# A graph-attention layer on one core: new order of the first loads, the query product in column tiles, and another order of the last frame's scores

## The chip, the cores and the metric

The kernel runs on one NeuronCore of a Trainium2 chip, as a single launch. TensorE (PE in the profile) multiplies matrices and writes to PSUM; VectorE (DVE), ScalarE (ACT) and GpSimd (POOL) do the elementwise work; SyncE (SP) issues nearly all DMAs. Each engine runs its own list of instructions in order, and they wait for each other by semaphores. The metric is the time on the device in microseconds, as the median of several runs.

## The reference, cut to what matters

For 16 frames (B) of 512 rows (N) and 512 features (F), with one query row of 512 numbers per frame:

```python
row_zero = v.sum(-1) == 0
q_exp = jnp.where(row_zero[..., None], 0.0, q[:, None, :])
self_feat = concatenate([v, q_exp], -1) @ W_self.T + b_self      # W1 acts on v, W2 on q
output = self_feat
for d in range(2):                                               # two directions of the edges
    A = adj_f if d == 0 else swapaxes(adj_f, 1, 2)
    cond, vb = A[:, :, :20].sum(-1), A[:, :, :20] @ w_bias + b_bias
    kv = self_feat[:, :20]                                       # 20 keys per frame
    qh, kh = self_feat @ Wq[d].T + bq[d], kv @ Wk[d].T + bk[d]   # 16 heads of 32
    aff = einsum('bnhd,bmhd->bnhm', qh, kh) / sqrt(32)
    w = softmax(where(cond > 0, aff, -9e15) + vb, axis=-1)
    out_t = einsum('bnhm,bmf->bnhf', w, kv)
    output = output + einsum('bnhf,hgf->bnhg', out_t, Wout[d]) + bout[d]
return v + relu(output)
```

## The kernel before

Every fp32 product is made from two parts of each operand: a high part (a copy by ACT, `wkh`, `w1h`, `woh`, `xh`) and a low part (the difference, `wkl`, `w1l`, `wol`, `xl`), and three products of them (`parts`, lines L513 to L515). A copy to the high part is ACT's, the subtraction for the low part is DVE's or POOL's.

**Prologue** (about the first 72 us). SP issues all loads in one list. PE first runs 11 products of ones (`warm`), then `query`: the 16 query rows times W2, as four plain fp32 products of `qT` (16 columns per chunk of 128 features) that add up in one PSUM bank. `key_self_feat` follows: the sums of the keys' rows (L443, L444), the query turned into columns by four transposes (L436, after ACT has copied it as `qrow`), and the keys' self features for all 16 frames, 320 columns (16 times 20), as 48 products into four banks of `aff`: first chunks 0 and 1 of the features for all four outputs f, then chunks 2 and 3 for one f after the other. DVE multiplies the query into the rows that are not zero (`sfkv`, L1082), adds the products (`key_feat`, L1091), ACT makes the high part with the bias (`key_feat_high`, L811), DVE the low one (`key_feat_low`, L1099). `keys` multiplies them by Wk: 32 products with `wkh` and 16 with `wkl`, then four groups of 12, each of which waits until DVE has taken a bank (`key`, L1054). `values` multiplies them by Wout and needs `wol` of chunk f at its f-th step, and all but one of the keys taken. Then come the first frame's self features and its products of keys and Wq (`g`).

**Frames.** The lists of all engines are written out by hand, so that frame n = b+1's self features are computed beside frame b's softmax. A frame has four tiles of 128 rows; a tile's `scores` are 24 products with 320 columns (3.5 us), for which the two banks of `aff` serve in turn. After a tile's scores DVE adds the bias and takes the maximum (`shift`, L1033 and L1035), POOL subtracts the maximum (`sub_max`, L1265), ACT takes the exponential (L882), DVE sums and inverts (`total`), POOL multiplies (`normalise_rest`, `normalise`). PE transposes the weights and multiplies them by the values (`attend_rest`, `attend`). DVE then adds the self features (`add_sf`, L1017), ACT applies the ReLU (`relu`), POOL issues a DMA that adds x in place (`add_x`, L1293), and SP stores the result one frame later (`store_out`, L367).

`ahead` is the number of frames that are still to come, at most 2: it is 1 in frame 14 and 0 in frame 15. The last frame has a list of its own: its tile 3 is scored in two halves (`last_scores`), DVE subtracts that tile's maximum itself (`last_sub_max`) and normalises it (`last_normalise`), and the result is stored in four parts (L405) as it comes.

## Time and profile before

| | us |
|---|---|
| median of 3 runs | 594.58 (592.99 to 594.88) |
| profiled execution, time | 593.21 |
| profiled execution, span of the core | 591.4 |
| PE busy in the span | 580.8 (98%) |
| DVE, POOL, ACT busy | 448.6, 439.5, 413.2 |

The span reaches from the first to the last instruction of the core; the rest of an execution's time lies around it. PE is busy in 98% of the span, and the chain of work that ended last is PE's for 92% of it. The granted clock is 1.0 of full speed in the whole of the span but its last slice.

### The profile page before, as it was taken

How to read it: one execution, taken by the hardware profiler on the slowest of the kernel's cores; microseconds unless marked ns; L12 is line 12 of the kernel's file. 1: busy time of each engine (PE TensorE's matmuls, PEld its weight loads, DVE VectorE, ACT ScalarE, POOL GpSimd, SP SyncE). 2: the span in 40 equal slices, each digit the busy share in tenths (PEclk: the TensorE clock that was granted, in tenths of full speed). 3: DMA queues.
4: the chain of work that ended last, by engine and by line, in shares of the span. 5: the costliest groups of instructions: out<-in, count | busy, mean ns of one | idle time of the engine just before them, and what ended most of it. 6: DMA issues, size and time to landing. Idle time of an engine off the chain costs nothing.

```text
span 591.4 us, 11118 instructions
## 1 busy us (share of the span) xinstructions
PE 580.8 (98%) x4303; PEld 495.3 (84%) x4303; DVE 448.6 (76%) x646; ACT 413.2 (70%) x829; POOL 439.5 (74%) x400
## 2 busy tenths in 40 slices
PE   8999999999999999999999999999999999999994
PEld 5977798888888888888888897979888888888882
DVE  4894876897778688777778786868977777777776
ACT  4738656787777798676778786868876767876542
POOL 0311299876898986699997589898668989867963
PEclk9999999999999999999999999999999999999999
DMA  8985462466385958267675646767643857491335
GB/s 307 430 318 137 115 181 86 134 159 177 112 239 152 225 168 232 74 192 190 201 197 155 210 148 144 252 158 222 190 124 126 218 172 232 149 236 47 71 107 185
DMA packets 39573, 106.04 MB, mean 179 GB/s; under 512 B 9184, under 2 KB 23008, under 8 KB 33120
## 3 DMA queue, kind: packets, MB, share of 16 engines
q1 hardware_dynamic: 37360, 89.60, 47.2%
q0 software_dynamic: 2160, 15.73, 13.9%
q8 instruction: 34, 0.56, 0.4%
q14 instruction: 19, 0.16, 0.1%
HBM read 85.84 MB, written 19.47 MB: 178 GB/s over the span
## 4 chain that ended last, share of the span: by engine, by line
PE 92%; DVE 3%; POOL 3%; DMA 1%; issue 0%; ACT 0%; DVEq 0%; SPq 0%; ACTq 0%
PE aff L582 36%; PE gen L513 10%; PE gen L515 10%; PE gen L514 10%; PE aff L549 8%; PE tp L596 4%; PE gen L643 3%; PE gen L653 2%; PE gen L596 1%; PE tp L513 1%; POOL z L1265 1%; PE tp L514 1%; PE tp L515 1%; DVE wol L1104 1%; DMA qT<-in_qT 1%; PE gen L429 1%
## 5 line engine op out<-in xcount | busy, mean ns | idle before, releaser
L1265 POOL TENSOR_TENSOR z<-z,mx 128x640 f32<-128x640 f32 x63 | 87.2, 1384 | 42.2 <-DVE mx L1035 42.1
L582 PE MATMUL aff<-gh,sfh 128*128 128x320 f32 x504 | 117.6, 315 | 0.0
L582 PE MATMUL aff<-gl,sfh 128*128 128x320 f32 x504 | 114.8, 309 | 0.0
L582 PE MATMUL aff<-gh,sfl 128*128 128x320 f32 x504 | 114.8, 309 | 0.0
L1253 POOL TENSOR_TENSOR z<-cb,bx 128x640 f32<-128x640 f32 x64 | 102.2, 1696 | 11.1 <-PE tp L515 10.2
L882 ACT ACTIVATE z<-z 128x640 f32<-128x640 f32 x63 | 46.6, 740 | 84.9 <-POOL z L1265 84.1
L513 PE MATMUL gen<-xh,w1h 128*128 128x512 f32 x256 | 104.1, 407 | 0.1
L515 PE MATMUL gen<-xh,w1l 128*128 128x512 f32 x256 | 101.2, 395 | 0.0
L514 PE MATMUL gen<-xl,w1h 128*128 128x512 f32 x256 | 101.2, 395 | 0.0
L1033 DVE TENSOR_TENSOR z<-aff,z 128x640 f32<-128x640 f32 x63 | 51.9, 824 | 61.2 <-PE aff L582 61.1
L1250 POOL TENSOR_TENSOR sfl<-sff,sfh 128x512 fp32r<-128x512 f32 x48 | 64.6, 1496 | 41.9 <-ACT sfh L749 41.9
L582 PEld LDWEIGHTS aff<-gh,sfh 128*128 128x128 f32 x504 | 83.2, 188 | 12.7 <-issue 12.6
L744 ACT ACTIVATE prod<-msk,wb 128x160 f32<-128x160 int32 x176 | 90.2, 589 | 0.0
L582 PEld LDWEIGHTS aff<-gh,sfl 128*128 128x128 f32 x504 | 84.3, 188 | 0.0
L582 PEld LDWEIGHTS aff<-gl,sfh 128*128 128x128 f32 x504 | 84.2, 188 | 0.0
L1246 POOL TENSOR_TENSOR xl<-x,xh 128x512 fp32r<-128x512 f32 x48 | 63.8, 1343 | 24.7 <-ACT xh L724 24.7
L975 DVE SCALAR_TENSOR_TENSOR sff<-nz,qb,gen 128x512 f32<-128x512 f32 x64 | 47.5, 745 | 30.5 <-PE gen L515 25.1
L1277 POOL TENSOR_TENSOR z<-z,rcp 128x512 f32<-128x512 f32 x63 | 67.0, 1064 | 4.9
L988 DVE TENSOR_TENSOR gl<-aff,gh 128x480 fp32r<-128x480 f32 (+1 forms) x96 | 51.3, 591 | 11.3 <-ACT gh L761 11.3
L513 PEld LDWEIGHTS gen<-xh,w1h 128*128 128x128 f32 x256 | 48.1, 188 | 11.6 <-DVE sff L975 0.3
L515 PEld LDWEIGHTS gen<-xh,w1l 128*128 128x128 f32 x256 | 48.1, 188 | 11.5
L514 PEld LDWEIGHTS gen<-xl,w1h 128*128 128x128 f32 x256 | 48.2, 188 | 9.5
(160 smaller groups left out, 1104.1 us busy)
## 6 DMA issues: line engine op xcount, KB each, us to landing
x<-in_x SPq DMA_DIRECT2D x16, 1024.0 KB, 4.7
xn<-in_xn SPq DMA_DIRECT2D x31, 512.0 KB, 4.7
sff<-in_x POOLq DMA_DIRECT2D x15, 1024.0 KB, 9.9
out_y<-sff SPq DMA_DIRECT2D x15, 1024.0 KB, 4.9
msk<-in_mask SPq DMA_DIRECT2D x16, 880.0 KB, 5.2
cb<-c_scratch SPq DMA_DIRECT2D x16, 320.0 KB, 3.8
nz<-nz_scratch SPq DMA_DIRECT2D x16, 256.0 KB, 3.5
wkT<-in_wkT SPq DMA_DIRECT2D x4, 512.0 KB, 8.2
```

The lines of the kernel that those rows point to most:

```text
L513: nc.tensor.matmul(acc, lh, rh, start=first, stop=False)
L514: nc.tensor.matmul(acc, lh, rl, start=False, stop=False)
L515: return nc.tensor.matmul(acc, ll, rh, start=False, stop=last)
L582: mm = nc.tensor.matmul(aff[:, t % 2, half, 0:SH], s, g[:, b - starts[group(b)], f, half * SH:(half + 1) * SH], start=(f == 0 and i == 0), ...
L744: last = nc.scalar.activation(prod[:, :, :, l], msk[:, :, :, :, l].rearrange("p t d m -> p t (d m)"), ACT.Copy, scale=wb[:, l:l + 1])
L988: lo = nc.vector.tensor_tensor(g_part(gl, pair, u, r), g_bank(pair, u, r), g_part(gh, pair, u, r).bitcast(F32), ALU.subtract)
L1033: nc.vector.tensor_tensor(zt, aff[:, t % 2, :, 0:SH], zt, ALU.add).then_inc(s_z, 1)
L1246: nc.gpsimd.tensor_tensor(xl[:, c, :], x[:, c, :], xh[:, c, :].bitcast(F32), ALU.subtract).then_inc(s_xl, 1)
L1250: nc.gpsimd.tensor_tensor(sfl[:, f, :], sff[n % 3][:, f, :], sfh[:, f, :].bitcast(F32), ALU.subtract).then_inc(s_sfl2, 1)
L1253: nc.gpsimd.tensor_tensor(z[slot][:, t, :].rearrange("p (q e) -> p q e", q=QG), cb[:].rearrange("p (q e) -> p q e", q=QG), bx[:, t].rearra ...
L1265: nc.gpsimd.tensor_tensor(zt(slot, t), zt(slot, t), heads(mx, t, M), ALU.subtract).then_inc(s_sub, 1)
L1277: nc.gpsimd.tensor_tensor(z[slot][:, t, 0:HG * P].rearrange("p (g m) -> p g m", m=MA), zt(slot, t)[:, :, 0:MA], heads(rcp, t, MA), ALU.mul ...
```

## The change

1. **Loads.** SP issues the keys' x (`kvx`) first, then the four pieces of W1, and only then W2, the query `qT` and `ident`. All else keeps its place. `qT` is padded with zeros from 16 to 32 columns per chunk, 64 KB instead of 32.
2. **Query.** The four products of the query no longer add up in PSUM: each writes 32 rows of its own of the bank (a column tile). ACT copies 128 rows, four full transposes follow, and DVE sums the four parts while it takes them (`qb`, now a reduction over 256 elements per partition). On PE the query now stands behind the 24 products of chunks 0 and 1, and its transposes behind the first six products of chunks 2 and 3.
3. **Keys' self features.** A comparison with zero on its own (in `c4`), then a multiplication for each f: two by DVE, two by POOL. On ACT `key_feat_high(0)` and `(1)` stand one place further ahead. `wk_low(0)` goes behind all of the key features on DVE.
4. **Low part of Wout.** Chunk 3 goes from DVE to POOL, behind `x_low` of chunks 0 and 1, with a semaphore of its own; chunk 2 is made after key group 6 instead of before it.
5. **Last frame.** Tile 1's scores of frame 15 are computed before frame 14's `attend_rest` and `attend`. On DVE frame 14's `add_sf`, and on ACT its `relu`, go behind frame 15's first total and shift or exponential 1. POOL takes `sub_max` of tile 1 ahead of its wait for `attend`, and issues `add_x(14)` after `sub_max` of tile 2. Tile 3's shift, exponential and sum are done in halves.

The diff, cut:

```diff
@@ sync
+            sp.dma_start(kvx[:], a["kvx"]).then_inc(s_kvx, 16)
+            for c in range(FC):
+                sp.dma_start(w1raw[:, c], a["w1T"][:, c]).then_inc(s_w1[c], 16)
             sp.dma_start(w2T, a["w2T"]).then_inc(s_w2, 16)
             sp.dma_start(qT[:], a["qT"]).then_inc(s_q_in, 16)
-            sp.dma_start(kvx[:], a["kvx"]).then_inc(s_kvx, 16)
             sp.dma_start(ident[:], a["ident"]).then_inc(s_id, 16)
-            for c in range(FC):
-                sp.dma_start(w1raw[:, c], a["w1T"][:, c]).then_inc(s_w1[c], 16)
@@ tensor
                 for c in range(FC):
-                    mm = nc.tensor.matmul(gen[0:B, 0, :], qT[:, c, :], w2T[:, c, :], start=(c == 0), stop=(c == FC - 1))
+                    mm = nc.tensor.matmul(gen[c * DH:(c + 1) * DH, 0, :], qT[:, c, :], w2T[:, c, :], start=True, stop=True)
...
                 for f in range(FC):
-                    mm = nc.tensor.transpose(gen[:, 0, f * B:(f + 1) * B], qrow[:, f * P:(f + 1) * P], ident[0:B, 0:B])
+                    mm = nc.tensor.transpose(gen[:, 0, f * P:(f + 1) * P], qrow[:, f * P:(f + 1) * P], ident[:])
...
-                query_columns()
...
+                query()
                 pe.wait_ge(s_w1l, FC)
                 for f in range(FC):
                     for c in range(2, FC):
                         mm = sums(f, c)
                     mm.then_inc(s_sfk, 1)
+                    if f == 0:
+                        query_columns()
...
-                    if n == 0:
+                    if n == 0 and f < FC - 1:
                         pe.wait_ge(s_wol, f + 1)
+                    elif n == 0:
+                        pe.wait_ge(s_wol3, 1)
...
-            query()
             key_self_feat()
...
-                    scores(b, slot, group(b), range(1, T - 1))
+                    scores(b, slot, group(b), range(2, T - 1))
...
-                scores(n, 1 - slot, group(n), range(1))
+                scores(n, 1 - slot, group(n), range(2 if ahead == 1 else 1))
@@ scalar
-                if c == 0:
-                    act.wait_ge(s_q, 1)
-                    nc.scalar.activation(qrow[:], gen[0:B, 0, :], ACT.Copy).then_inc(s_qrow, 1)
+            act.wait_ge(s_q, 1)
+            nc.scalar.activation(qrow[:], gen[:, 0, :], ACT.Copy).then_inc(s_qrow, 1)
...
+            key_feat_high(0)
             wk_high(2)
-            key_feat_high(0)
+            key_feat_high(1)
             wk_high(3)
-            key_feat_high(1)
...
-                exponential(b, slot, 1)
+                    exponential(b, slot, 1)
+                    for j in range(HG):
+                        relu(b - 1, 1 - slot, j)
+                else:
+                    exponential(b, slot, 1)
...
+                    for half in range(2):
+                        zt = z[slot][:, T - 1, half * SH:(half + 1) * SH]
+                        act.wait_ge(s_sub3, half + 1)
+                        nc.scalar.activation(zt, zt, ACT.Exp).then_inc(s_exp, 1)
@@ vector
-            dve.wait_ge(s_qb, 1)
-            for f in range(FC):
-                nc.vector.scalar_tensor_tensor(sfkv[:, f], gen[:, 1, 0:KV].rearrange("p (b m) -> p b m", m=M), 0.0,
-                                               qb[:, f, :].unsqueeze(2).to_broadcast([P, B, M]), ALU.not_equal, ALU.mult).then_inc(s_kvq, 1)
+            nc.vector.tensor_scalar(c4[:].rearrange("p b m -> p (b m)"), gen[:, 1, 0:KV], 0.0, None, ALU.not_equal).then_inc(s_kvm, 1)
...
+            dve.wait_ge(s_qt, 1)
+            nc.vector.tensor_reduce(qb[:], gen[:, 0, :].rearrange("p (f c b) -> p f b c", f=FC, c=FC)[:, :, 0:B, :], AX_X, ALU.add).then_inc(s_qb, 1)
...
-            for c in range(1, FC):
+            for c in range(FC):
                 wk_low(c)
             for g in range(GD):
                 key(g)
-                if g >= 3 and g < GD - 1:
+                if g == 3 or g == 4:
                     wo_low(g - 3)
+                if g == GD - 2:
+                    wo_low(2)
@@ gpsimd
+            pool.wait_ge(s_kvm, 1)
+            pool.wait_ge(s_qb, 1)
+            for f in range(FC // 2, FC):
+                nc.gpsimd.tensor_tensor(sfkv[:, f], c4[:], qb[:, f, :].unsqueeze(2).to_broadcast([P, B, M]), ALU.mult).then_inc(s_kvq2, 1)
             pool.wait_ge(s_wkl, FC)
-            for c in range(FC):
+            for c in range(2):
+                x_low(0, c)
+            pool.wait_ge(s_woh, FC)
+            nc.gpsimd.tensor_tensor(wol[:, FC - 1], woT[:, FC - 1], woh[:, FC - 1].bitcast(F32), ALU.subtract).then_inc(s_wol3, 1)
+            for c in range(2, FC):
                 x_low(0, c)
```

The lists of two engines in the prologue show where the query and the key features go. Ahead of the keys, DVE had (line, operation, out<-in, shape; names as above, the comparison's result stands in `c`):

```order
L1071 TENSOR_TENSOR kvl<-kvx,kvh 128x320 x4
L1075 TENSOR_TENSOR w1l<-wself,w1h 128x512
L1078 COPY qb<-gen 128x64
L1075 TENSOR_TENSOR w1l<-wself,w1h 128x512 x3
L1082 SCALAR_TENSOR_TENSOR sfkv<-gen,qb 128x320 x4
L1085 TENSOR_TENSOR bosum<-bo 128x4
L1095 TENSOR_TENSOR wkl<-wkT,wkh 128x1024
L1091 TENSOR_TENSOR sfkv<-sfkv,aff 128x320 x2
L1099 SCALAR_TENSOR_TENSOR sfkvl<-sfkv,bself,sfkvh 128x320
```

and has now:

```order
L1093 TENSOR_TENSOR kvl<-kvx,kvh 128x320 x4
L1097 TENSOR_TENSOR w1l<-wself,w1h 128x512 x4
L1099 TENSOR_SCALAR c<-gen 128x320
L1101 TENSOR_TENSOR bosum<-bo 128x4
L1103 TENSOR_REDUCE qb<-gen 128x64
L1109 TENSOR_TENSOR sfkv<-c,qb 128x320
L1118 TENSOR_TENSOR sfkv<-sfkv,aff 128x320
L1109 TENSOR_TENSOR sfkv<-c,qb 128x320
L1118 TENSOR_TENSOR sfkv<-sfkv,aff 128x320
L1126 SCALAR_TENSOR_TENSOR sfkvl<-sfkv,bself,sfkvh 128x320
```

Two of the four multiplications have left DVE, and the first `wkl` has gone behind this piece: all four of them now stand behind the last `sfkvl`.

On ACT, the copies to the high parts of Wk and of the key features stood in this order:

```order
L807 ACTIVATE wkh<-wkT 128x1024 x3
L811 ACTIVATE sfkvh<-sfkv,bself 128x320
L807 ACTIVATE wkh<-wkT 128x1024
L811 ACTIVATE sfkvh<-sfkv,bself 128x320 x3
L825 ACTIVATE woh<-woT 128x1024 x2
```

and now stand so:

```order
L811 ACTIVATE wkh<-wkT 128x1024 x2
L815 ACTIVATE sfkvh<-sfkv,bself 128x320
L811 ACTIVATE wkh<-wkT 128x1024
L815 ACTIVATE sfkvh<-sfkv,bself 128x320
L811 ACTIVATE wkh<-wkT 128x1024
L815 ACTIVATE sfkvh<-sfkv,bself 128x320 x2
L829 ACTIVATE woh<-woT 128x1024 x2
```

The first two key features are copied one piece of Wk sooner each.

In the last frame POOL had, from the subtraction for tile 0 on (`z<-z,mx` is `sub_max`, `zr` and `z<-z,rcp` the normalising, the DMA is `add_x(14)`):

```order
L1265 TENSOR_TENSOR z<-z,mx 128x640
L1269 TENSOR_TENSOR zr<-z,rcp 128x128
L1277 TENSOR_TENSOR z<-z,rcp 128x512
L1265 TENSOR_TENSOR z<-z,mx 128x640
L1293 DMA sff<-in_x 128x2048
L1265 TENSOR_TENSOR z<-z,mx 128x640
L1269 TENSOR_TENSOR zr<-z,rcp 128x128
```

and has now:

```order
L1302 TENSOR_TENSOR z<-z,mx 128x640 x2
L1306 TENSOR_TENSOR zr<-z,rcp 128x128
L1314 TENSOR_TENSOR z<-z,rcp 128x512
L1306 TENSOR_TENSOR zr<-z,rcp 128x128
L1314 TENSOR_TENSOR z<-z,rcp 128x512
L1302 TENSOR_TENSOR z<-z,mx 128x640
L1330 DMA sff<-in_x 128x2048
```

The DMA that adds x to frame 14 has gone from behind the second subtraction to behind the third. DVE, in the same frame, had:

```order
L1017 TENSOR_TENSOR sff<-gen,sff 128x512 x2
L1017 TENSOR_TENSOR sff<-tp,sff 128x512 x2
L1048 TENSOR_REDUCE rcp<-z 128x32
L1050 RECIPROCAL rcp<-rcp 128x32
L1033 TENSOR_TENSOR z<-aff,z 128x640
L1035 TENSOR_REDUCE mx<-z 128x32
L1033 TENSOR_TENSOR z<-aff,z 128x640
L1035 TENSOR_REDUCE mx<-z 128x32
```

and has now:

```order
L1070 TENSOR_REDUCE rcp<-z 128x32
L1072 RECIPROCAL rcp<-rcp 128x32
L1055 TENSOR_TENSOR z<-aff,z 128x640
L1057 TENSOR_REDUCE mx<-z 128x32
L1039 TENSOR_TENSOR sff<-gen,sff 128x512 x2
L1039 TENSOR_TENSOR sff<-tp,sff 128x512 x2
L1070 TENSOR_REDUCE rcp<-z 128x32
L1072 RECIPROCAL rcp<-rcp 128x32
```

The four additions of self features to frame 14 (`sff`) have gone behind frame 15's first total and its shift of tile 1.

## Rows read from the trace of the kernel before

**Rows 1.** What PE waited for, whole span: us, times, longest

```profile
PE tp L614 <- POOL z L1277: 2.1, 1, 2.1
...
PE gen L429 <- DMA qT<-in_qT: 0.7, 1, 0.7
PE tp L513 <- DVE wself L1054: 0.7, 1, 0.7
```

**Rows 2.** PE in time: start, us, line, out<-in, count [idle before]

```profile
1.04 4.13 PE L415 MATMUL tp<-ones_r 128*128 128x512 f32 x11 [1.04 <-DVE ones_r L1065]
5.91 3.61 PE L429 MATMUL gen<-wself,qT 128*16 128x512 f32 x8 [0.73 <-DMA qT<-in_qT]
...
11.18 0.41 PE L513 MATMUL aff<-kvh,w1h 128*128 128x320 f32 x1
...
18.32 0.31 PE L471 MATMUL gen<-sfkvh,wkh 128*128 128x320 f32 x1
...
25.72 0.41 PE L513 MATMUL gen<-sfkvh,wkh 128*128 128x320 f32 x1 [0.20 <-DVE wself L1054]
...
33.75 0.49 PE L513 MATMUL tp<-woh,sfkvh 128*120 128x512 f32 x1 [0.72 <-DVE wself L1054]
...
47.90 1.28 PE L494 MATMUL aff<-bk,bqd 128*32 128x320 f32 x16
```

**Rows 3.** DVE in time, prologue

```profile
7.90 1.70 DVE L1071 TENSOR_TENSOR kvl<-kvx,kvh 128x320 fp32r<-128x320 f32 x4 [5.89 <-ACT kvh L797]
...
20.30 0.55 DVE L1099 SCALAR_TENSOR_TENSOR sfkvl<-sfkv,bself,sfkvh 128x320 fp32r<-128x320 f32 x1 [0.17 <-ACT sfkvh L811]
20.77 3.49 DVE L1095 TENSOR_TENSOR wkl<-wkT,wkh 128x1024 fp32r<-128x1024 f32 x3
...
31.38 1.85 DVE L1104 TENSOR_TENSOR wol<-woT,woh 128x1024 fp32r<-128x1024 f32 x1
...
33.62 1.21 DVE L1104 TENSOR_TENSOR wol<-woT,woh 128x1024 fp32r<-128x1024 f32 x1
```

**Rows 4.** ACT in time, prologue

```profile
7.40 1.55 ACT L797 ACTIVATE kvh<-kvx 128x320 fp32r<-128x320 f32 x4 [5.38 <-DMA kvx<-in_kvx]
...
15.77 1.06 ACT L807 ACTIVATE wkh<-wkT 128x1024 fp32r<-128x1024 f32 x1 [0.22 <-DMA wkT<-in_wkT]
...
17.18 1.05 ACT L807 ACTIVATE wkh<-wkT 128x1024 fp32r<-128x1024 f32 x1
```

**Rows 5.** POOL in time, prologue

```profile
25.13 7.02 POOL L1246 TENSOR_TENSOR xl<-x,xh 128x512 fp32r<-128x512 f32 x4 [24.69 <-ACT xh L724]
```

**Rows 6.** DVE in time, last frame

```profile
565.63 1.29 DVE L1017 TENSOR_TENSOR sff<-gen,sff 128x512 f32<-128x512 f32 x2 [0.41 <-PE tp L653]
...
572.93 0.82 DVE L1033 TENSOR_TENSOR z<-aff,z 128x640 f32<-128x640 f32 x1 [1.84 <-PE aff L582]
...
577.54 0.88 DVE L1000 TENSOR_TENSOR z<-z,mx 128x640 f32<-128x640 f32 x1
578.35 0.81 DVE L1048 TENSOR_REDUCE rcp<-z 128x32 f32<-128x640 f32 x1
```

**Rows 7.** POOL in time, last frame

```profile
572.39 0.88 POOL L1293 DMA_DIRECT2D sff<-in_x  x1
574.70 1.27 POOL L1265 TENSOR_TENSOR z<-z,mx 128x640 f32<-128x640 f32 x1 [1.44 <-DVE mx L1035]
575.94 0.66 POOL L1269 TENSOR_TENSOR zr<-z,rcp 128x128 f32<-128x128 f32 x1
576.68 1.06 POOL L1277 TENSOR_TENSOR z<-z,rcp 128x512 f32<-128x512 f32 x1
```

**Rows 8.** SP in time, last frame: the stores of frames 14 and 15

```profile
580.41 0.34 SPq L367 DMA_DIRECT2D out_y<-sff  x1
586.63 2.06 SPq L405 DMA_DIRECT2D out_y<-sff  x4
```

**Rows 9.** Busy time by stretch: the last two columns are DMA share, GB/s

```profile
589.00:590.00 1.00, 0.00 (x0) 0.00 (x0) 0.00 (x0) 0.00 (x0) 0.00 (x0) 1.00 1.04 381
```

More of the change, by code:

```diff
@@ L114, in build @@
             [("bsrow", [P, F], F32)],
-            [("qrow", [B, F], F32)],
+            [("qrow", [P, F], F32)],
             [("gap", [P, FC * N], F32)],
@@ L910, in batch @@
                 if ahead == 0:
-                    act.wait_ge(s_sub3, 1)
-                    nc.scalar.activation(z[slot][:, T - 1, :], z[slot][:, T - 1, :], ACT.Exp).then_inc(s_exp, 1)
+                    for half in range(2):
+                        zt = z[slot][:, T - 1, half * SH:(half + 1) * SH]
+                        act.wait_ge(s_sub3, half + 1)
+                        nc.scalar.activation(zt, zt, ACT.Exp).then_inc(s_exp, 1)
                     for c in LAST_ORDER[::2]:
@@ L951, in batch @@
                 exponential(n, other, 0)
-                for j in range(HG):
-                    relu(b, slot, j)
+                if ahead >= 2:
+                    for j in range(HG):
+                        relu(b, slot, j)
             batches(batch)
@@ L995, in last_evict_wt, with last_sub_max, last_total, last_reciprocal @@
                 nc.vector.tensor_copy(wt(B - 1, c), wt_bank(B - 1, c).rearrange("p (t q) -> p t q", t=T)).then_inc(s_wt3, 1)
-            def last_sub_max(b, slot, t):
-                dve.wait_ge(s_mx, b * T + T + 1)
-                zt = z[slot][:, t, :].rearrange("p (g m) -> p g m", m=M)
-                nc.vector.tensor_tensor(zt, zt, mx[:, t, :].unsqueeze(2).to_broadcast([P, D * QG, M]), ALU.subtract).then_inc(s_sub3, 1)
+            def last_sub_max(b, slot, half):
+                t, heads = T - 1, slice(half * QG, (half + 1) * QG)
+                dve.wait_ge(s_mx, b * T + T + half)
+                zt = z[slot][:, t, half * SH:(half + 1) * SH].rearrange("p (g m) -> p g m", m=M)
+                nc.vector.tensor_tensor(zt, zt, mx[:, t, heads].unsqueeze(2).to_broadcast([P, QG, M]), ALU.subtract).then_inc(s_sub3, 1)
+            def last_total(b, slot, half):
+                t, heads = T - 1, slice(half * QG, (half + 1) * QG)
+                dve.wait_ge(s_exp, b * T + T + half)
+                nc.vector.tensor_reduce(rcp[:, t, heads], z[slot][:, t, half * SH:(half + 1) * SH].rearrange("p (g m) -> p g m", m=M),
+                                        AX_X, ALU.add).then_inc(s_sum, 1)
+            def last_reciprocal(b):
+                dve.wait_ge(s_sum, b * T + T + 1)
+                nc.vector.reciprocal(rcp[:, T - 1, :], rcp[:, T - 1, :]).then_inc(s_rcp, 1)
             def last_normalise(b, slot, t):
@@ L1104, in wo_low @@
                 nc.vector.tensor_tensor(wol[:, c], woT[:, c], woh[:, c].bitcast(F32), ALU.subtract).then_inc(s_wol, 1)
-            wk_low(0)
+            key_query(0)
             key_feat(0)
+            key_query(1)
             key_feat(1)
@@ L1192, in batch @@
                 shift(b, slot, 1)
-                if ahead >= 1:
-                    x_low(n, FC - 1)
-                shift(b, slot, 2)
-                total(b, slot, 1)
                 if ahead == 0:
+                    for j in range(HG):
+                        add_sf(b - 1, other, j)
+                    total(b, slot, 1)
+                    shift(b, slot, 2)
                     last_shift(b, slot, 0)
+                    last_sub_max(b, slot, 0)
                     last_shift(b, slot, 1)
-                    last_sub_max(b, slot, 3)
+                    last_sub_max(b, slot, 1)
                     total(b, slot, 2)
-                    total(b, slot, 3)
+                    last_total(b, slot, 0)
+                    last_total(b, slot, 1)
+                    last_reciprocal(b)
                     last_normalise(b, slot, 3)
@@ L1209, in batch @@
                     return
+                x_low(n, FC - 1)
+                shift(b, slot, 2)
+                total(b, slot, 1)
                 shift(b, slot, 3)
@@ L1236, in batch @@
                 shift(n, other, 0)
-                for j in range(HG):
-                    add_sf(b, slot, j)
+                if ahead >= 2:
+                    for j in range(HG):
+                        add_sf(b, slot, j)
             batches(batch)
@@ L1323, in batch @@
                         x_low(n, 1)
+                    if ahead == 0:
+                        sub_max(b, slot, 1)
                     pool.wait_ge(s_pv, b * HG)
@@ L1326, in batch @@
                     normalise(b, slot, 0)
-                    sub_max(b, slot, 1)
-                    if ahead == 0:
-                        pool.wait_ge(s_ya, (b - 1) * 16)
-                        add_x(b - 1)
                     if ahead >= 1:
+                        sub_max(b, slot, 1)
                         x_low(n, 2)
-                sub_max(b, slot, 2)
+                if ahead >= 1:
+                    sub_max(b, slot, 2)
                 normalise_rest(b, slot, 1)
                 normalise(b, slot, 1)
+                if ahead == 0:
+                    sub_max(b, slot, 2)
+                    pool.wait_ge(s_ya, (b - 1) * 16)
+                    add_x(b - 1)
                 if ahead >= 1:
```

20 lines of the change are left out of this document (13 added, 7 removed).

## The prediction

> **What bounds the kernel now.** I read first the table of waits of PE, then the order in time of each engine in the first 50 us and in the last 30, and last the stretches of DMA at the end. PE is busy for 98% of the span. The table of waits shows how little is left to take: one wait of 2.1 us in the last frame, one of 0.7 for the query's data, one of 0.7 in the keys and values [rows 1]. So a change saves time only where it takes work off PE, fills one of these waits, or shortens the ends where PE doesn't set the pace. This change works at both ends, and leaves frames 1 to 13 as they are.
>
> **Prologue, PE's side.** The query costs 3.61 us for four plain fp32 products of 512 columns, 0.90 each [rows 2]. The same form as the new one stands in the trace: eight fp32 products of 128 by 32 with 320 columns take 1.28 [rows 2]. Four side by side are one round: a round of 320 columns is 0.90 times 320/512 = 0.56, two rounds are 1.13, and 0.15 is left for starting and draining, so the query should take 0.90 + 0.15 = 1.05. It leaves the front of the list, where PE had also waited 0.73 for it. The page "TensorEngine Tiling (Array Packing)" of the Trainium skill, section "Key Properties", says that a change of tiling mode drains TensorE, which speaks against a place between full products; it would be the 0.15 above, and no more, since the row was taken between full products too.
>
> When can the sums begin? W2 and qT (1056 KB) have landed when PE starts at 5.91, kvx (640 KB more) when ACT starts at 7.40 [rows 2, 4]: 640 KB in 1.49 us. With kvx first it lands about 5.91 minus 416 KB at that rate, at 4.9. From kvx's start on ACT to the last `kvl` were 2.2 us (7.40 to 7.90 + 1.70) [rows 3, 4]. Then come `w1l` and the products, say 0.7: 4.9 + 2.2 + 0.7 = 7.8 instead of 11.18. The 48 products of sums took 7.14 (11.18 to 18.32), 0.149 each [rows 2]. Now: 24 of them to 11.4, query to 12.4, six to 13.3, transposes about 0.5 to 13.8, and 18 to 16.5. PE has the sums 1.8 us sooner than at 18.32.
>
> **What the keys wait for.** I don't take these 1.8 us, since they meet a stream of loads that keeps its place. Everything ahead of Wk is the same data, plus 32 KB. ACT waited for the third piece of Wk until 15.77, and took the fourth at 17.18 [rows 4]. With the new order ACT does: piece 2, to 15.5; key feature 0 (0.5, by what lies between the third piece's end and 17.18), to 16.0; piece 3 to 17.0; feature 1 to 17.5; piece 4 to 18.5; features 2 and 3 to 19.5. The last `sfkvl` on DVE follows to 20.0, against 20.30 + 0.55 = 20.85 before [rows 3]. But DVE now has all four `wkl` behind it instead of three: 3.49/3 = 1.16 each [rows 3], 20.0 + 4.65 = 24.65, against 20.77 + 3.49 = 24.26 before. PE's last four products with `wkl` wait for the fourth, and the next group starts about 0.85 later, at 25.5 against 25.72 [rows 2]. **Gain 0.2**, with 0.8 saved by the features and 1.16 paid for the fourth `wkl`, and PE's old slack lost. Bounds: nothing, if ACT or DVE are 0.2 later than this; 1.0, if Wk lands a little sooner.
>
> **Values.** PE waited 0.72 at 33.75 for DVE, which was in `wol` from 31.38 to 33.2 and took key group 6 behind it [rows 2, 3]. The four groups of 12 products take 48 times 0.149 = 7.1: from 25.5 to 32.6. Group 6 is done by PE at 25.5 + 36 times 0.149 = 30.9, and DVE takes it then, ahead of `wol` 2. So PE goes on at 32.7, not 33.75: **gain 0.9 more, 1.05 together**. What could be late next: `wol` 2 ends at about 31.8 + 1.85 = 33.6, PE wants it six values' products on, of 512 columns and so 0.149 times 1.6 = 0.24 each: 32.7 + 1.4 = 34.1. POOL's chunk 3 stands behind two `x_low` of 7.02/4 = 1.76 each, from 25.13: 28.7, plus two such for twice the size, 32.2 [rows 5]; PE wants it at 34.8. `wol` took 1.85 beside POOL and 1.21 without it [rows 3], and I used the long one. POOL's `x_low` 3 now ends near 35.7; SP issues the next x, and the keys' store behind it, only then. PE had no wait at all from 33.75 to the last frame [rows 1], so I count this at nothing; if its cover were gone it would cost the 0.4 by which 35.7 is later than the last key's end.
>
> **Last frame, the engines.** The work on PE is the same, tile 1's 3.5 us only change places with frame 14's attend. DVE gets tile 1 sooner, but now has frame 14's four `add_sf` (2 times 1.29, less overlap 2.4 [rows 6]) behind the shift. My order in time: exponential 0 at 567.3 (an estimate; it was there when `add_sf` let DVE go at 568.0), total 0 (0.81 and a reciprocal, 1.1) to 568.5, shift 1 to 570.1, `add_sf` to 572.5, total 1 to 573.6, shift 2 (twice 0.82) to 575.2, two half shifts of 0.9 and two half subtractions of 0.45 to 578.0. Before, shift 2 began at 572.93 and total 2 at 578.35 [rows 6]. So total 2, and all that follows it up to the last additions, comes 0.35 to 0.4 sooner.
>
> **Last frame, the DMAs.** `add_x(14)` was issued at 572.39, and `store_out(14)`, which waits for it, at 580.41: 8.0 us [rows 7, 8]. Now POOL does `sub_max` 1 (1.27) to 571.4, the two multiplications (0.66 + 1.06) [rows 7] to 573.1, waits for total 1, again two to 575.4, `sub_max` 2 to 576.7, and then issues it. The store of frame 14 (1 MB) can start at 584.7. At 381 GB/s [rows 9] that is 2.75 us, behind an estimated 0.6 of start: to 588.0. The last frame's four stores, issued from 586.63 to 588.69 [rows 8], will be issued from 586.2 and stand behind it: 588.0 + 2.75 = 590.75, where without it they ended near 586.63 + 0.9 + 2.75 = 590.3 (0.9 from issue to data is an estimate, by DMA's full share up to 590). So the end moves from a gain of 0.4 to a **loss of 0.4**. I take 0.3, since at the front of the queue a part may run faster. The page "DMA: Bandwidth & Descriptors" of the Trainium skill, section "Queues, rings and completion order", has a completion land only after every earlier write of that DMA engine; by that rule the last stores can't be reported ahead of frame 14's, and the tail is +0.4; were stores to pass each other, it would be -0.4.
>
> **Sum.** -1.05 + 0.3 = -0.75. Against the profiled execution, 593.21 (span 591.4): 592.4. The median of the three runs lies 1.4 above it, so 594.58 - 0.8 = **593.8**. The three runs spread from 592.99 to 594.88; 0.3% is 1.8 us, and less than that this kernel's measurement cannot tell from no change.
>
> **Rivals.**
> - *The stores do not collide* (add_x lands in less than 7 us, or stores overlap): -1.05 - 0.4 = -1.45, 593.1. For it: the moved DMA finds less other traffic. Against: 8.0 us in a stretch where it was almost alone. Chance 0.22.
> - *The query's whole saving arrives.* PE's sums are 1.8 sooner; if Wk's pieces landed sooner as well, or ACT overtook them, the keys would end up to 1.8 to 3 sooner: with the values' 0.9 and the tail, about -2.8, 591.8. Against: ACT's wait for the third piece at 15.77. Chance 0.15.
> - *Slower: the clock of PE falls in the new gap at the front.* The eleven products of ones ran at 4.13/11 = 0.375 each, where one of 512 columns takes 0.24 later (0.149 for 320 columns): this was largely the lower level, 1.2 GHz, before PE had been at work. Now PE has only the eight small products between 5.2 and 7.8, where it had the query. If the clock fell there, the first 24 sums would take 7.1 instead of 3.6, the features come about 3.5 later and, less the 0.5 to 1 that they have in hand, the keys too: +2.7 - 0.75, 596.5. It decides if more than some 12 of these products run at the lower level. Against: before, 0.73 of idleness at 5.2 left the clock up. Chance 0.08.
> - *The forecast*, chance 0.55, own range 592.9 to 594.7.
>
> **Numbers.** Forecast and first rival lie within 0.3%, but for the first rival's lower part (0.05) and a share of the forecast's for spread of runs (0.06); with 0.13 of the second, faster by over 0.3% has 0.24. Slower has the clock's 0.08. The rest, 0.68, is within 0.3%. The range reaches down to the second rival, 591.8, and up to 595.4, which is prologue at nothing, tail at +0.4, and 0.4 for the runs; it leaves out about 0.15.
>
> **What would show it.** `kvl` done near 7.1, PE's sums from about 7.8, query of about 1.05 in its new place. The last `sfkvl` near 20.0, the fourth `wkl` near 24.6, and PE's group 4 at 25.5. No wait before the values, which start at 32.7. POOL's DMA at 576.7, the store of frame 14 at 584.7, the last four from 586.2 less the prologue's 1.05, all ends close on each other at 380 to 400 GB/s. It would be wrong if Wk landed at other times than 15.77 and 17.18, if PE's first products showed the lower level, or if `x_low` held up the first frame.

## The result, and the profile after

The changed kernel takes **599.19 us** (median of 6, 596.09 to 601.06), the kernel before 594.48 in the same job (6 runs, 592.99 to 594.88): a ratio of 1.0077, 95% interval 1.006 to 1.0094. It is slower by 0.8%: the forecast of 593.8 was wrong in sign too, and the median lies above the whole range (591.8 to 595.4). The profiled execution took 596.09 (span 594.2) and is the fastest of the six, so 3 us of the median are not in its trace.

What PE waited for, in the table of waits after (against [rows 1]):

```profile
PE tp L620 <- POOL z L1314: 2.4, 1, 2.4
PE aff L555 <- ACT c L856: 1.9, 1, 1.9
...
PE gen L475 <- ACT wkh L811: 0.5, 1, 0.5
PE gen L481 <- DVE wkl L1122: 0.3, 1, 0.3
```

The second row is new, and it is the largest wait outside the last frame. It stands in none of the stretches that the forecast spoke of: L555 is the first of `key_products(0, 0)`, 20 us behind the values. PE in time (start, us, line, out<-in, count, idle time before) shows the front end (against [rows 2]), and this wait at its end:

```profile
1.04 5.00 PE L416 MATMUL tp<-ones_r 128*128 128x512 f32 x11 [1.04 <-DVE ones_r L1087]
7.74 0.41 PE L519 MATMUL aff<-kvh,w1h 128*128 128x320 f32 x1 [0.28 <-DVE w1l L1097]
12.14 1.07 PE L430 MATMUL gen<-wself,qT 128*32 128x512 f32 x8 [0.61 <-DMA qT<-in_qT]
17.86 0.39 PE L475 MATMUL gen<-sfkvh,wkh 128*128 128x320 f32 x1 [0.49 <-ACT wkh L811]
25.36 0.56 PE L481 MATMUL gen<-sfkvh,wkl 128*128 128x320 f32 x2 [0.28 <-DVE wkl L1122]
26.42 0.42 PE L519 MATMUL gen<-sfkvh,wkh 128*128 128x320 f32 x1 [0.20 <-DVE wself L1076]
...
54.03 2.02 PE L555 MATMUL aff<-bd,wq 64*128 64x80 f32 x32 [1.90 <-ACT c L856]
```

Who is late is read backwards, from ACT to SP to POOL. ACT copies the first `c` at 53.57; ahead of that, before it could place the keys' blocks (`bd`), it waited 3.83 us for `khc`, the keys read back from scratch memory:

```profile
49.75 1.91 ACT L760 ACTIVATE bd<-khc 32x320 f32<-32x320 f32 x4 [3.83 <-DMA khc<-kh_scratch]
53.57 0.41 ACT L856 ACTIVATE c<-aff 128x320 f32<-128x320 f32 x1
```

In the kernel before the same two lines stood 4.06 and 4.04 us earlier, with no wait at `bd`:

```profile
45.69 1.89 ACT L755 ACTIVATE bd<-khc 32x320 f32<-32x320 f32 x4
49.53 0.42 ACT L852 ACTIVATE c<-aff 128x320 f32<-128x320 f32 x1
```

SP, before and then after, issues the next frame's x, the keys' halves to scratch, and, once these have landed, `khc` (start, time, line):

```profile
32.17 0.33 SPq L271 DMA_DIRECT2D x<-in_x  x1
35.31 0.81 SPq L324 DMA_DIRECT2D kh_scratch<-wself  x2
37.77 0.32 SPq L278 DMA_DIRECT2D nz_scratch<-nzc  x1
42.82 0.32 SPq L289 DMA_DIRECT2D khc<-kh_scratch  x1
```

```profile
36.13 0.33 SPq L272 DMA_DIRECT2D x<-in_x  x1
36.51 0.91 SPq L325 DMA_DIRECT2D kh_scratch<-wself  x2
37.90 0.59 SPq L279 DMA_DIRECT2D nz_scratch<-nzc  x1
47.50 0.32 SPq L290 DMA_DIRECT2D khc<-kh_scratch  x1
```

The store itself is issued only 1.2 us later than before, but `khc`, which waits for it to land, 4.7 us later. What did move by 4 us is the x ahead of it, and x waits for POOL's `x_low` (against [rows 5]):

```profile
25.73 2.56 POOL L1283 TENSOR_TENSOR xl<-x,xh 128x512 fp32r<-128x512 f32 x2 [8.42 <-ACT xh L729]
29.13 2.51 POOL L1342 TENSOR_TENSOR wol<-woT,woh 128x1024 fp32r<-128x1024 f32 x1 [0.84 <-ACT woh L832]
31.60 4.50 POOL L1283 TENSOR_TENSOR xl<-x,xh 128x512 fp32r<-128x512 f32 x2
```

So: `wol` 3 on POOL (2.51, and 0.84 of waiting for ACT's `woh`) ends the four `x_low` at 36.10 instead of 32.15; `c` is 4.04 late; of that 2.16 was slack (before, `c` had been copied by 49.95, and the products began 2.16 later, at 52.11, with no wait, as PE's row of before shows), and 1.9 is left as PE's wait.

```profile
52.11 1.57 PE L549 MATMUL aff<-bd,wq 64*128 64x80 f32 x24
```

At the other end (against [rows 6] to [rows 8]), DVE with the two half shifts and half subtractions up to total 2, POOL with `add_x(14)`, and SP with the last stores:

```profile
576.98 0.48 DVE L1064 TENSOR_TENSOR z<-aff,z 128x320 f32<-128x320 f32 x1
577.49 0.49 DVE L1066 TENSOR_REDUCE mx<-z 128x16 f32<-128x320 f32 x1
578.01 0.98 DVE L1012 TENSOR_TENSOR z<-z,mx 128x320 f32<-128x320 f32 x1
...
580.36 0.81 DVE L1070 TENSOR_REDUCE rcp<-z 128x32 f32<-128x640 f32 x1
...
578.59 0.87 POOL L1330 DMA_DIRECT2D sff<-in_x  x1
...
586.59 0.34 SPq L368 DMA_DIRECT2D out_y<-sff  x1
588.64 2.39 SPq L406 DMA_DIRECT2D out_y<-sff  x4
```

The last stores go out 2.0 us later than before, 1.9 of it by PE's wait at the key products, and from there the span lasts 594.2 - 588.64 = 5.6 us, where it lasted 591.4 - 586.63 = 4.8. Span by span: 1.9 (the wait), 0.1 (the rest up to the last stores), 0.8 (the stores), 2.8 in all. The medians lie 4.7 apart. The changed kernel's lies 3.1 above its profiled execution, and the kernel before's 1.3 above its own (594.48 and 593.21), so about 1.8 us of the loss are in no trace yet. The six executions differ in their clock: their times and mean granted clocks were 596.09 (0.999), 596.35 (0.999), 598.84 (0.993), 599.54 (0.988), 600.07 (0.993) and 601.06 (0.990).

### The profile page after: what moved, and what is told of

The parts are those of the page before. It is cut to its first block, busy times and chain, and to the rows that moved or that the text cites. A ratio compares the mean times of both kernels' runs of the same rounds, so it can differ in the third digit from the quotient of the medians.

```text
span 594.2 us, 11126 instructions
## 1 busy us (share of the span) xinstructions
PE 580.4 (98%) x4303; PEld 495.4 (83%) x4303; DVE 448.6 (76%) x646; ACT 413.0 (70%) x830; POOL 443.5 (75%) x403
## 4 chain that ended last, share of the span: by engine, by line
PE 83%; DMA 5%; POOL 4%; DVE 3%; ACT 2%; SPq 1%; issue 1%; DVEq 0%; ACTq 0%
PE aff L588 35%; PE gen L519 10%; PE gen L521 9%; PE gen L520 9%; PE aff L555 8%; PE tp L602 4%; DMA x<-in_x 3%; PE gen L649 2%; PE gen L659 2%; DMA kh_scratch<-wself 2%; POOL z L1302 1%; POOL xl L1283 1%; PE gen L602 1%; DVE z L1055 1%; POOL z L1314 1%
## 5 line engine op out<-in xcount | busy, mean ns | idle before, releaser
L1290 POOL TENSOR_TENSOR z<-cb,bx 128x640 f32<-128x640 f32 x64 | 102.3, 1696 | 11.2 <-PE tp L521 10.2
L519 PEld LDWEIGHTS gen<-xh,w1h 128*128 128x128 f32 x256 | 48.1, 188 | 11.6 <-DVE sff L986 0.3
L1070 DVE TENSOR_REDUCE rcp<-z 128x32 f32<-128x640 f32 x63 | 51.2, 812 | 6.9 <-ACT z L886 6.9
```

The costliest lines, as they stand in the source:

```text
L519: nc.tensor.matmul(acc, lh, rh, start=first, stop=False)
L1290: nc.gpsimd.tensor_tensor(z[slot][:, t, :].rearrange("p (q e) -> p q e", q=QG), cb[:].rearrange("p (q e) -> p q e", q=QG), bx[:, t].rearra ...
```

## The experiments

**One part at a time.** `e_last` is the kernel before with part 5 alone; `e_front` the changed kernel without parts 4 and 5; `e_wo3` the kernel before with part 4 alone; `e_xlow` the changed kernel with all four `x_low` ahead of `wol` 3 on POOL:

```diff
             pool.wait_ge(s_wkl, FC)
-            for c in range(2):
+            for c in range(FC):
                 x_low(0, c)
             pool.wait_ge(s_woh, FC)
             nc.gpsimd.tensor_tensor(wol[:, FC - 1], ...).then_inc(s_wol3, 1)
-            for c in range(2, FC):
-                x_low(0, c)
```

Expected of `e_last`:

> The kernel before with part 5 alone (order of the last frame). Theory A (frame 14's store now runs into the last four stores; the engines gain nothing): PE ends at most 0.2 earlier or later than before, the last store lands 0.6 to 1.0 later, the kernel is 0.7 to 1.0 us slower. Rival B (the last frame costs nothing, all of the loss of 4.7 is at the front): within 0.2 us of before.

Expected of `e_front`:

> The changed kernel with parts 4 and 5 undone: only the loads, the query in column tiles and the keys' features are new. Theory A (the front moves the keys 0.7 later, and what PE loses is that alone): 0.7 to 1.0 us slower than before, PE waits again before the values, no wait at the first products of keys and Wq. Rival B (the new gaps of PE at the front bring its clock down in some executions): some runs show a granted clock near 0.99 and are 3 to 5 us slower.

Expected of `e_wo3`:

> The kernel before with part 4 alone (chunk 3 of Wout's low part on GpSimd ahead of two low parts of x; chunk 2 behind key group 6). Theory A: values start 0.8 earlier, SP issues the next x at 35 to 35.5 instead of 32.2, the keys' store lands 3 to 4 us later, PE waits 1.5 to 2.5 us at the first products of keys and Wq: 0.8 to 1.5 us slower. Rival B (the late x is hidden here): 0.8 us faster.

Expected of `e_xlow`:

> The changed kernel with one line moved: GpSimd makes all four low parts of x before chunk 3 of Wout's low part. Theory A (the 1.9 us wait at the first products of keys and Wq comes from the late next x and the keys' store behind it): SP issues x near 33 instead of 36.1, the wait is gone, PE gets 1.9 us back, about 0.9 us slower than before remains in the undisturbed runs. Rival B (the keys' store takes 10 us for another reason, as its later start): the wait stays above 1 us.

Measured, beside before at 594.34 in the same job:

| kernel | median us (runs) | ratio, 95% interval |
|---|---|---|
| `e_last` | 594.81 (594.07 to 595.89, 10) | 1.0008 [0.9999, 1.0017] |
| `e_front` | 594.52 (593.45 to 595.34, 10) | 1.0006 [0.9995, 1.0016] |
| `e_wo3` | 598.13 (595.82 to 598.67, 5) | 1.0054 [1.0036, 1.0073] |
| `e_xlow` | 595.29 (594.96 to 596.22, 10) | 1.0016 [1.0007, 1.0026] |

Part 4 alone carries most of the loss, 3.8 of the 4.7 us, more than the 0.8 to 1.5 expected of `e_wo3`. Its place on POOL is the reason: in `e_xlow`, with all four `x_low` ahead, x is issued at 32.66 and `khc` at 43.25, PE doesn't wait at the key products (it waits 0.34 for `wol` 3 in the values instead), and the loss against before falls from 4.7 us to 0.95. `e_last`, 0.5 above before, lies between its two expectations, and its interval still holds no change. `e_front` missed its 0.7 to 1.0 in the median, though its trace reaches the key products 0.9 later than before (52.99 for 52.11).

The trace of `e_wo3`, an execution at 598.67, also shows a part of the loss that the first trace lacked. PE in time, and then the stretches behind it (from and to, length, busy time of PE, its weight loads, DVE, ACT and POOL, granted clock, DMA share, GB/s):

```profile
53.15 3.20 PE L551 MATMUL aff<-bd,wq 64*128 64x80 f32 x32 [1.87 <-ACT c L854]
```

```profile
52.00:54.00 2.00, 0.85 (x13) 0.86 (x14) 2.00 (x3) 2.00 (x5) 0.31 (x1) 0.93 0.28 60
54.00:56.00 2.00, 2.00 (x22) 2.00 (x20) 1.14 (x2) 2.00 (x6) 2.00 (x2) 0.50 0.12 14
56.00:58.00 2.00, 2.00 (x8) 1.57 (x7) 1.30 (x4) 2.00 (x7) 0.19 (x1) 0.50 0.58 159
58.00:60.00 2.00, 2.00 (x6) 1.52 (x6) 0.39 (x1) 1.04 (x3) 0.00 (x0) 0.50 0.82 260
60.00:62.00 2.00, 2.00 (x19) 1.50 (x19) 0.69 (x1) 0.00 (x0) 0.00 (x0) 0.86 0.65 182
```

Behind a wait of 1.87 us TensorE is granted half its clock, 1.2 GHz, from about 54 to 60, and the same 32 key products take 3.20 us instead of the 2.02 of the trace after. From the first key products to the transposes of the last frame this trace needs 532.4 us (53.15 to 585.54), the kernel before 529.3 (52.11 to 581.43): the lower level costs 3.1 us. The page "TensorE: Matmul & The Clock Gate" of the Trainium skill, Part 1, has the clock set by how busy PE has lately been, over windows that run free of the program, so that one kernel differs from run to run. The traces agree that it differs from run to run: after the changed kernel's wait of 1.90 the clock stayed full, after this one of 1.87 it did not. The same page of the Trainium skill, in the table of "Why this matters for your kernels", warns of longer idle stretches than these; here the measured fall decides.

**The x load ahead of the store.** `e_kh` is the changed kernel with SP's two steps exchanged, POOL's order left as changed:

```diff
             sp.wait_ge(s_xl, FC)
-            load_x(1)
             ...the keys' halves to kh_scratch...
+            load_x(1)
             store_nonzero(0)
```

> The changed kernel, with SP's load of x(1) moved behind the store of the keys' halves to scratch. POOL keeps the changed order (third low part of the output weights ahead of the last two x_low). Theory (the store lands late, 10.3 us against 6.3, because the x load was put in the drained queues just ahead of it and its 16 KB-per-row pieces are served first): the store lands in 5 to 7 us, khc is loaded by 44, c is copied by 51, PE waits under 0.3 us at the first key products, and the time is 594.5 to 596 us; x(1) lands later and something of the next frame may wait for it. Rival (the landing is slow because the queues were empty, or for the store's own sake): landing still over 9 us, PE waits over 1 us there, and the time is 597 to 599 us.

Measured: 594.86 (594.04 to 595.17, 10 runs) beside 594.49, 1.0006 [0.9996, 1.0016]. (The "16 KB per row" in this theory is wrong: 1024 KB over 128 rows are 8 KB each.) SP in time:

```profile
34.94 0.81 SPq L322 DMA_DIRECT2D kh_scratch<-wself  x2
35.79 0.90 SPq L272 DMA_DIRECT2D x<-in_x  x1
37.39 0.58 SPq L279 DMA_DIRECT2D nz_scratch<-nzc  x1
40.90 0.32 SPq L290 DMA_DIRECT2D khc<-kh_scratch  x1
```

The store lands in 4.9 us (6.3 before, 10.3 after), `khc` is even earlier than before, PE doesn't wait at the key products, and the loss is down to 0.4 us, which the interval doesn't tell from nothing, though POOL's `x_low` is still late (it ends at 35.61, x is issued at 35.79). Where x stands ahead, `khc` follows the issue of x by 10.65 (before), 11.37 (after), 10.59 (`e_xlow`) and 11.29 (`e_wo3`), and by 10.2 to 11.6 in all 16 traces, while the store stood 0.4 to 3.1 us behind x: it is x's issue that sets when the store lands. The page "DMA: Bandwidth & Descriptors" of the Trainium skill, "Queues, rings and completion order", has a completion land only behind every earlier write of the same DMA engine; the four distances agree. The rule gives only the order: x itself landed 6.6 to 7.3 us after its issue in these four, `khc` went out 3.3 to 4.8 us after that, and no run shows what took this time.

`e_xlow` and `e_kh` keep everything of the changed kernel but the late store, and none of their 20 executions lies above 596.3. So the changed kernel's executions at 598.8 and more come with the late store and its wait, and not with the new front end or the last frame, which these two versions have as well.

**Filling the wait.** Products of ones ahead of the first key products, eight (`e_fill`; `e_fill_look` is a further execution of it) and eleven (`e_fill11`). `after_look` and `after_more` are further executions of the changed kernel as it is:

```diff
+            for _ in range(8):
+                nc.tensor.matmul(aff[:, 1, 1, :]..., ones_r[:], ..., start=True, stop=True)
             pe.wait_ge(s_c4, 1)
             key_products(0, 0, True)
```

> The changed kernel, with eight products of a 128x128 weight of ones by 512 columns put on PE just ahead of its wait for the first c of key products(0, 0), where it stood idle for 1.90 us. Their results go to a bank that is written anew before it is read, so the output is the same. Theory (the idle stretch ahead of the first key products, besides its 1.9 us, brings TensorE's clock down in some executions): the eight products take about 8 x 0.22 = 1.8 us of the wait, the key products still start at about 54.0, the granted clock is full around 50 to 60 in all executions, and times lie between 596 and 597 us with none at 599 or above. Rival (the executions at 599 to 601 us have another cause, such as the last frame's waits or the chip): the same spread as the changed kernel, a median of 598 to 599.5 us.

> The changed kernel with eight products ahead of the first key products, for the trace of another execution: two of its four times were 599.5 and 599.9 us although the wait is filled. Theory (the clock falls in these all the same, because the 0.5 us that PE still waits, or the work before it, is enough): an execution near 599.5 us shows the granted clock near 0.5 for some microseconds behind 50 and no longer wait. Rival (the wait itself is longer there): the granted clock is full and PE waits 3 us or more at the first key products. An execution near 596.5 us tells neither.

> The changed kernel with eleven products of 512 columns ahead of the first key products; eight took 1.99 us and left PE 0.53 us idle. Theory (the idleness brings the clock down, and 0.5 us of it can still be enough): PE doesn't wait there, key products begin at about 54.2 to 54.5, and all times lie at 595 to 598 us (those at the upper end by the last frame's own loss of the clock). Rival (the executions near 600 us have another cause): times of 599 us and more in about half of the executions, with PE busy there throughout.

> The changed kernel itself, for the trace of another of its executions: four of its six times were 598.8 to 601.1 us and the trace so far is of one at 596.09. Theory (those executions lose TensorE's clock behind the wait at the first key products): in an execution at 598.8 us or more the granted clock is near 0.5 for some microseconds behind 54 and PE's work of the second and third frame is some 3 us longer for it, with the same wait of 1.9 us. Rival (something waits longer in those executions, such as the keys' store): the wait at the first key products is 4 us or more, and the granted clock there is full.

> The changed kernel again, for more of its times with their clocks and one more trace. Theory: times fall into groups by the mean granted clock: 596 to 596.4 at 0.999, near 597.5 at 0.994 where only the last frame loses the clock (about 1.3 to 1.5 us, as the traces of other kernels show), 599 to 601 where it is lost behind the first key products. Rival: times of 599 us and more at a mean clock of 0.997 or above.

Measured: `e_fill` 596.45, 596.57, 599.49 and 599.93, with 0.53 us of wait left in the trace at 596.57; `e_fill_look` 598.07 with the same 0.53 and a full clock there (its loss was the last frame's, 0.50 at 586 to 588); `e_fill11` 596.62, 597.00, 597.52 and 597.67, no wait. `after_look` took 596.22 at a mean clock of 0.999, so it can't tell its two expectations apart. `after_more` gave 596.24 (0.998), 599.22 (0.988), 600.01 (0.993) and 602.37 (0.985). Of the changed kernel's eleven executions seven lie at 598.8 or above, of the four with the wait wholly filled none. PE in time in `e_fill11`:

```profile
52.07 2.67 PE L675 MATMUL aff<-ones_r 128*128 128x512 f32 x11
54.67 2.02 PE L555 MATMUL aff<-bd,wq 64*128 64x80 f32 x32
```

Eight products missed their expectation of none at 599 or above; eleven met theirs. Four runs are few, and there is no trace of an execution of `e_fill` or of the changed kernel near 600 us. The half clock behind this wait is shown for part 4 alone; that it is also behind the changed kernel's executions at 598.8 and more is what their clocks (0.985 to 0.993), `e_xlow`, `e_kh` and `e_fill11` speak for, no more. The two of `e_fill` at 599.5 and 599.9, with but half a microsecond left, stay unexplained.

**The last frame.** `e_nostore` is `e_last` without frame 14's store; its output for frame 14 is left out.

> The kernel before with the last-frame part alone, and without frame 14's store (frame 14's output is left out). It is to be read against the last-frame part alone, whose span was 0.9 us longer than before's at the same clock though PE was hardly longer. Theory (frame 14's store now shares the queues with the last frame's last stores): without it the last stores land 0.7 to 1.0 us sooner after the last attend, the span is 592.0 to 592.3 at a clock of 0.994 to 0.999 and the median is 0.7 to 1.0 us below that of the last-frame part alone, 593.8 to 594.1 us. Rival (the last frame's engines or PE's own idle time made it longer): the median stays at 594.8 us and the last stores still land 5.8 to 6 us after the last attend.

Measured: 594.57 (593.37 to 596.10, 10 runs) beside 594.49, 1.0007 [0.9995, 1.002]: not the 0.8 us less that was expected. The traces show where the store does and doesn't matter. From the issue of the last stores to the end of the span it is 4.8 us before and in `e_nostore` (594.3 - 589.54). Where frame 14's store is issued 2.0 to 2.2 us ahead of the last ones it is 5.6 to 6.1 (the three traces of the changed kernel, and 5.8 in `e_fill11`); where it is 3.3 to 3.7 ahead, 4.8 to 5.0 in four of five traces and 5.8 in one (`e_xlow`). The two issues stand further apart where the last frame itself takes longer, by the clock. These are the stretches of `e_last` behind PE's wait of 2.4:

```profile
580.00:582.00 2.00, 0.54 (x5) 0.55 (x6) 1.93 (x4) 0.00 (x0) 1.92 (x3) 1.00 0.96 201
582.00:584.00 2.00, 1.93 (x14) 1.12 (x11) 1.67 (x3) 1.09 (x2) 0.73 (x2) 0.69 0.93 193
584.00:586.00 2.00, 2.00 (x11) 0.50 (x10) 0.00 (x0) 0.60 (x1) 0.00 (x0) 0.50 0.38 135
```

From the transposes to the last stores it takes 6.7 us here (581.46 to 588.12) and 5.2 before (581.43, where its wait of [rows 1] ends, to 586.63, [rows 8]): 1.5 us for the lower level. The changed kernel at full clock takes 5.2 too (583.45 to 588.64). `e_wo3x` below, whose last frame is that of the kernel before, takes 6.7 (580.72 to 587.40) with the clock at 0.51 from 582 to 584; by their mean clocks of 0.994 to 0.997 many executions of the kernel before have this loss too, of which the profiled one had none. So the collision and the loss of clock seem to take each other's place: at a mean clock of 0.998 or more the median of `e_last` is 0.95 us above before's (594.29, 3 executions, and 593.34, 9), at a lower one 0.4 (594.90, 7, and 594.47, 17), while `e_nostore` at 0.998 or more is 0.35 above (593.67, 3, and 593.32, 6). These groups are small, and no run changes the one without the other.

**Versions meant to be faster.** `e_wo3x` is the kernel before with `wol` 3 on POOL behind all four `x_low`. `e_tail` and `e_tail18` add to it 30 and 18 products of 128 columns in the last frame's wait; `e_fillb` is the kernel before with the 18 products alone:

```diff
                     start_sum(b, slot, 3)
+                    for _ in range(18):
+                        nc.tensor.matmul(wt_bank(b, 0)[:, (T - 1) * P:T * P], identr[:], identr[:], start=True, stop=True)
                     last_transposes(b, slot, 2)
```

> The kernel before with the third low part of the output weights given to GpSimd, but only after it has made all four x_low. Theory (the part saves VectorE's time ahead of the values and costs only where it makes x_low late): values start at 32.9 to 33.2 where they started at 33.75, the next x and the keys' store are issued within 0.5 us of before's 32.17 and 35.31, PE doesn't wait at the first key products, and the time is 0.5 to 0.9 us below before, 593.5 to 593.9 us (ratio 0.9985 to 0.9992). Rival (what the values gain is given back at a later wait for the low part itself, or in the fold): within 0.3 us of before.

> The third low part of the output weights made by GpSimd behind all four x_low, and 30 products of 128 columns put on PE in the last frame, just ahead of its wait of 2.03 us for the third row tile's scores (their results are written anew before they are read). Theory (in the executions at a mean clock of 0.994 to 0.997 that wait brings the clock down, which makes the last attends about 1.5 us longer): the clock stays full to the last attend, the mean clock is 0.999 in nearly all executions, and the median falls to 592.6 to 593.4 us, 1 to 2 us below before (ratio 0.997 to 0.998). Rival (the clock falls there in as many executions, whatever fills the wait): median 594.2 to 594.7, mean clock 0.994 in most.

> As the run with 30 products in the last frame's wait, but with 18. The 30 took 3.3 us from start to start of the next, where the wait was 2.03, so that the transposes came 1.3 us late; 18 take 18 x 0.11 = 2.0 us. Theory (the filling keeps the clock, and its excess was what it cost): mean clock 0.997 or above in nearly all executions, and a median 1.0 to 1.4 us below that run's 594.19, thus 592.8 to 593.2 us and below before's by 0.6 us or more. Rival (with fewer products the clock falls again, or the time was lost elsewhere): median 594 us or more.

> The kernel before with nothing but 18 products of 128 columns in the last frame's wait of 2.05 us for the third row tile's scores. Theory (the last frame's loss of clock is in before's median, and filling the wait takes it away): mean clock 0.997 or above in nearly all executions, median 593.2 to 593.7 us, 0.6 to 1.1 us below before's in the same job. If the third low part on GpSimd behind x_low had given 0.7 of the gain of the run with both, this median lies 0.5 us or more above 593.49. Rival (the gain of that run came from the prologue): within 0.3 us of before.

| kernel | median us (runs) | before | ratio, 95% interval | mean clock |
|---|---|---|---|---|
| `e_wo3x` | 594.42 (593.66 to 595.35, 12) | 594.49 | 0.9999 [0.9988, 1.001] | 9 of 12 at 0.995 or less |
| `e_tail` | 594.19 (593.59 to 594.91, 12) | 593.82 | 1.0004 [0.9995, 1.0014] | 0.997 to 0.999 |
| `e_tail18` | 593.49 (592.90 to 593.85, 11) | 594.26 | 0.9988 [0.9979, 0.9996] | 0.997 to 0.999 |
| `e_fillb` | 593.23 (592.84 to 593.62, 12) | 594.51 | 0.9979 [0.9971, 0.9988] | 0.997 to 1.000 |

`e_wo3x` missed: its trace starts the values at 32.69 and reaches the last frame's transposes 0.7 us earlier (580.72), yet the median doesn't show it. `e_tail` kept the clock but missed its time: the 30 products held the transposes up, 3.3 us (579.10 to 582.40) for a wait of 2.03. `e_tail18` is 0.8 below before and 0.7 below `e_tail`, not 1.0. `e_fillb`, without `wol` 3 on POOL, is as fast, so the gain is the filler's. In time and by stretches:

```profile
579.50 2.12 PE L697 MATMUL tp<-identr 128*128 128x128 f32 x18
581.72 0.33 PE L614 MATMUL tp<-ident,z 128*128 128x128 f32 x1
```

```profile
580.00:582.00 2.00, 1.90 (x18) 1.76 (x18) 1.93 (x4) 0.00 (x0) 1.92 (x3) 1.00 0.35 139
582.00:584.00 2.00, 1.93 (x16) 1.27 (x18) 1.93 (x3) 1.20 (x3) 0.99 (x2) 1.00 0.95 393
584.00:586.00 2.00, 2.00 (x40) 0.40 (x36) 0.00 (x0) 0.48 (x1) 0.00 (x0) 1.00 0.00 0
```

The clock is full to the last attend, the wait has gone, and nothing is late for it. Eighteen useless products and no other edit make the kernel 0.2% faster than before, and its median is 1% below the changed kernel's 599.19, taken in another job.

## Why the prediction was wrong

**The step that failed** is the end of the paragraph on the values: "POOL's `x_low` 3 now ends near 35.7; SP issues the next x, and the keys' store behind it, only then ... I count this at nothing; if its cover were gone it would cost the 0.4". The first half was right (36.10, x at 36.13). The price was not: it compared x's new time with the last key's end, as if only the store's own issue mattered, and not with x's old time, 32.17. `khc` can be fetched only 10.2 to 11.6 us after x is issued, so it moved with x's 4 us, and `c` with it; the slack of 2.16, which I hadn't read, took its part and 1.9 came through. Absence of a wait in the table showed only that nothing was late, not how much slack there was. That is two thirds of the profile's loss; `e_xlow` and `e_kh`, which undo either link, show it.

**The clock** was given as a rival at the wrong place, the front gap, at 2.7 us. There it held: the 24 sums from 7.74 were done by 11.53 (12.14 less the query's wait of 0.61), as against a forecast of 11.4. (Its premise, that the products of ones ran at the lower level, rests on their duration of 0.375 alone: the granted clock reads 1.00 there in the trace of before.) It fell behind the new wait instead, at a cost of 3.1 us where traced. Nothing in the sum had a term for what a new wait does to the work behind it.

**The keys**: forecast 0.2 sooner (25.5), measured 26.42, 0.7 later. `kvl`, the sums (7.74 for 7.8) and the query (1.07 for 1.05) came as worked out, but the sum had no wait for `qT`, which now comes behind W1 and W2: PE waited 0.61 for it, the query ended at 13.21 and not 12.4, and ACT's copy of it, ahead of all pieces of Wk in ACT's list, at 13.88. So the last `sfkvh` ended at 20.2 and not 19.5, the last `sfkvl` at 20.76 and not 20.0, and the four `wkl` at 25.3 and not 24.65. The next group then started 1.1 us behind them, for the 0.85 of the sum. `e_front`, whose median is 0.2 above before, agrees with no gain.

**The values**: order and size nearly right. They start at 33.70 with no wait, 7.28 us after key group 4 where it was 8.03, so 0.75 of the 0.9 was gained, and 0.7 had gone into the keys; in `e_wo3`, with no change to the keys, they start at 32.97.

**The last frame**: +0.3 forecast. Total 2 came no sooner: up to the second shift's maximum all was as worked out, but the first half subtraction took 0.98 while POOL subtracted too (the second, with POOL idle, 0.49) where I had 0.45, and PE's wait grew from 2.05 to 2.40. The collision was right: the store of frame 14 was issued 8.0 us after `add_x`, and cost 0.8 at the end, as in the sum, where +0.8 and a gain of 0.4 by the engines made +0.4. It is this gain that was not there. Part 5 costs 0.5 in the median (`e_last`), which the interval doesn't quite tell from nothing.

**The baseline**: I set the median against the profile by a constant 1.4. Much of that is the last frame's loss of clock, which `e_fillb` takes away (1.3 us of the median): it is a cost that the profiled execution of before just didn't have.

## What to carry to other kernels

When a step is put ahead of another on an engine, follow everything behind it through the queues to the engine that sets the pace, and read the slack there, in us, from the trace: a missing wait doesn't say how much is left. A DMA that others wait for should be issued ahead of a large load that nobody needs yet, since in every trace here it landed behind that load. Where PE must wait 2 us in an otherwise full stream, products that nobody needs can be cheaper than the wait, if they are cut to its length: in the last frame 18 of them gained 1.3 us, and 30 gained nothing.

## What the runs showed of the hardware that was not expected

- A wait of 1.87 us with PE busy on both sides halved the granted clock for about 6 us and cost 3.1 us, in one trace; three traces with waits of 1.7 to 1.9 at the same place kept it. After waits of 2.0 to 2.4 in the last frame the loss of clock, where it came, cost 1.2 to 1.6 us, and 2.6 once.
- The keys' store, 640 KB in two pieces, landed in 4.9 us when issued ahead of a 1 MB load, and in 10.3 us when issued 0.4 us behind one.
- In the changed kernel one piece of `wol` on DVE took 2.97 us while POOL made its own piece (2.51), and the next 1.39 beside `x_low`; before, a piece took 1.85 beside `x_low` and 1.21 with POOL idle [rows 3].
